# Fifteen expert blocks beside the cross-attention instead of eleven, in groups that sum no batch

## The chip, the cores and the metric

The kernel runs on one core of one Trainium2 chip. The metric is the device time of one execution in microseconds (us); smaller is better. All data is float32. The program is written engine by engine: TensorE (PE) multiplies, ScalarE (ACT) takes exponentials and ReLUs, VectorE (DVE) does the small arithmetic, GpSimd (POOL) issues the DMAs of the expert blocks, and SyncE (SP) the other DMAs. The engines meet through semaphores.

## The reference

One decoder layer over x of 1024 rows by 128, with a context of 6404 rows by 96:

```python
x = x + _L0_attn_ref(_layernorm(x), Wqvk, Wo)                 # 16 heads of 8, causal
x = x + _L0_xattn_ref(_layernorm(x), ctx_768, Wq, bq, ...)    # 16 heads of 8, 6404 keys
x = x + _L0_ffn_ref(_layernorm(x), router_w, router_b, W1, b1, W2, b2)
# the last one: 8 experts, the 2 best of each row, softmax of their two scores as gates
#   h = relu(x @ W1[e] + b1[e])    (128 -> 512);    y = h @ W2[e] + b2[e]    (512 -> 128)
```

## The kernel before

**The cross-attention.** It takes most of the time. Queries are done in two halves of 512. For each half, the 16 heads are taken as 4 quads of 4 heads, and for each quad the keys as 50 tiles of 128. One tile gives 4 PSUM banks of scores (one a head, 128 keys by 512 queries). The banks are exponentiated in *groups*: `GROUPS[1]` has 505 of them, numbered 0 to 504, in the second half of 3 banks each. PE goes through them in `attention`: in turn `group` it waits for the exponential of `group` (`exp_done`), writes the scores of `group + 2` (line 1541), then sums each *batch* (the 4 banks of one tile) that this exponential completed, with the values (line 1577), and then runs what the table `beside` holds for that number. ACT does one exponential a group (line 826) and nothing else there. There are two sets of 3 PSUM banks, so scores are at most two groups ahead of ACT. As a group has 3 banks and a batch 4, in four groups in a row three complete one batch each and the fourth completes none; in the second half the fourth is the one whose number is 2 above a multiple of 4 (with one change of pattern at the end of each quad, groups 304, 371, 437 and 504, which complete two).

**The experts.** The first 512 rows are known after group 237 (`SUMMED_AT`). Their rows are normalised, routed, sorted by expert through DRAM into up to 15 blocks of 128 rows (`BLOCKS`), and each block is multiplied with the weights of its own expert. One block is two steps on PE: *hidden* (`hidden_of_block`, line 1804, 4 products 128x128x128) and *output* (`output_of_block`, line 1811, 4 products). Each is followed by work of another engine: ReLU with bias (`block_relu`, line 1335, on DVE), and a copy (`block_output`, line 1341, DVE). Blocks 0 to 10 (`EARLY` = 11) are done beside the second half of the cross-attention: block j has its hidden step in group `HIDDEN_AT + BLOCK_STEP * j` = 315 + 16 j, its output step 8 groups later. These are all groups that complete a batch. Before them, four steps (`turn_block_rows`) transpose the block rows in groups 297, 301, 305 and 309. Blocks 11 to 14 come after the attention (`late_hidden`, `late_output` on PE; `late_relu`, `late_output` on ACT, lines 878 and 750), in free PSUM banks.

**After the attention.** The second 512 rows have yet to be projected (`project_heads(2, 1, ...)`, line 1679), added to x and normalised on DVE (lines 1030, 916 to 937), transposed (line 1408) and copied (line 1036). PE runs this projection only after the hidden step of block 12. Then come all 8 experts densely on these 512 rows: 32 units of `hidden_units` (line 1868) and `expert_output` (line 1876) in a loop, ReLU on ACT (line 897), scaling by gates and summing on DVE (lines 1393, 1396). `first_half_together` gates and adds the first 512 rows at expert `MEET_AT`.

**Two branches.** Whether the cross-attention may be computed without a running maximum is decided on the chip: `choose` makes a branch of two programs, the one shown by the trace (`attention`) and a general one. In before, both join and the late blocks and dense experts are written once, behind the join.

POOL loads the weights of block j after the output step of block j - 2 (line 722 to 724), alternating between two places in `q_all`; the last two use parts of `k_ring`.

Of the kernel before, what the change touches and what calls it, by code (L numbers as in the profile page):

```python
# [25 lines left out]
P = 128  # L26
# [22 lines left out]
EARLY = 11  # L49
LATE_BANKS = (2, 4, 5, 6)  # L50
# [175 lines left out]
def ctxT_bank(c):  # L226
# [17 lines left out]
B2_AT, COUNT_AT, TURN_AT, HIDDEN_AT = (SUMMED_AT + n for n in (33, 37, 60, 78))  # L244
BLOCK_STEP, OUTPUT_STEP = 16, 8
# [3 lines left out]
MEET_AT = 3  # L249

BLOCK_STEPS = ([("biases", 0), ("counts", 0)] + [("turned", q) for q in range(-(-BLOCKS // 4))] +
               [(what, j) for j in range(EARLY) for what in ("hidden", "output")] + [("hidden", EARLY)] +
               [(what, j + n) for j in range(EARLY, BLOCKS - 1) for n, what in ((1, "hidden"), (0, "output"))] +
               [("output", BLOCKS - 1)])
# [16 lines left out]
def decoder_layer(nc, x, ctx, wqvk, wo_s, wq, bq, wk, bk, wv, bv, wo_x, bo, rw, rb, w1, b1, w2, b2, out):  # L271
    stack = ExitStack()
    with stack:
# [37 lines left out]
        k_space = k_ring[:, 2 * PIECE:2 * PIECE + 4 * HALF].bitcast(F32).rearrange("p (n c) -> p n c", c=HALF)  # L311
# [99 lines left out]
        def bank(b):  # L411
            return psum[:, b, :]
# [13 lines left out]
        for name in (  # L426
# [8 lines left out]
            "block_ps block_done picked experts_made xs_cleared rows_moved weights0 weights1 weights2 weights3 "  # L435
# [32 lines left out]
        OUTPUTS_STORED = ROWS_LOADED + 16 * 3  # L468
        OUTPUTS_BACK = OUTPUTS_STORED + 16 * 2 * 4

        def weights_of(j):

            if j < EARLY + 2:
                return q_space[:, j % 2 * 2], q_space[:, j % 2 * 2 + 1], s[f"weights{j % 2}"], 32 * (j // 2 + 1)
            n = j - EARLY - 2
            return k_space[:, 2 * n], k_space[:, 2 * n + 1], s[f"weights{2 + n}"], 32
# [157 lines left out]
        def _(pool):  # L634
# [63 lines left out]
            def to_experts(fast):  # L698
# [17 lines left out]
                for j in range(BLOCKS):  # L716
                    w1_at, w2_at, loaded, _ = weights_of(j)
                    if 2 <= j < EARLY + 2:
                        pool.wait_ge(s["block_ps"], block_step("output", j - 2))
                    elif j == EARLY + 2 and fast:  # L720
                        pool.wait_ge(L[1]["qk_done"], piece_scored(LOADS - len(PIECES)))
# [8 lines left out]
                pool.wait_ge(s["block_done"], block_step("output", BLOCKS - 1))  # L730
                store(EARLY, BLOCKS - EARLY)
# [5 lines left out]
            def general_cross():  # L737
                load_v_general(1)
                to_experts(False)
# [3 lines left out]
            choose(pool, 1, lambda: to_experts(True), general_cross)  # L743
# [4 lines left out]
        def _(act):  # L748
# [124 lines left out]
            act.wait_ge(s["experts_made"], 2)  # L873

            def late_relu(j):
                act.wait_ge(s["block_ps"], block_step("hidden", j))
                for f in range(NF):
                    ins = act.activation(block_hidden[j % 2][:, f * P:(f + 1) * P], bank(j % 2)[:, f * P:(f + 1) * P],
                                         ACT.Relu, bias=b1_blocks[:, j, f:f + 1])
                ins.then_inc(s["block_done"], 1)  # L880

            def late_output(j):
                act.wait_ge(s["block_ps"], block_step("output", j))
                evac(blocks[:, j, :], bank(LATE_BANKS[j - EARLY])[:, 0:D], s["block_done"])

            late_relu(EARLY)
            for j in range(EARLY + 1, BLOCKS):
                late_relu(j)
                late_output(j - 1)
            late_output(BLOCKS - 1)  # L890

# [512 lines left out]
        def _(pe):  # L1404
# [421 lines left out]
            def late_hidden(j):  # L1826
                if j - 2 >= EARLY:
                    pe.wait_ge(s["block_done"], block_step("hidden", j - 2))
                hidden_of_block(j, bank(j % 2))

            def late_output(j):
                pe.wait_ge(s["block_done"], block_step("hidden", j))
                output_of_block(j, bank(LATE_BANKS[j - EARLY])[:, 0:D])
# [97 lines left out]
```

## Time and profile before

| | |
|---|---|
| time before, median of 3 runs | 978.95 us (977.52 to 982.57) |
| the profiled execution | 975.13 us, span 973.4 us |
| ACT busy | 858.2 us (88%) |
| PE busy | 861.8 us (89%) |
| DVE busy | 183.2 us (19%) |
| POOL busy | 46.7 us (5%) |

The span runs from the first to the last recorded instruction; the execution's own time is 1.7 us longer. "Idle before" is time in which an engine had nothing running before an instruction, and "<-" names what ended it. The granted clock of TensorE is a share of 2.4 GHz: 1.00 is 2.4, and 0.50 is 1.2.

### The profile page before, as it was taken

What the parts mean: (1) busy time and instruction counts of PE and PEld (TensorE: products, weight loads), DVE (VectorE), ACT (ScalarE), POOL (GpSimd) and SP (SyncE); (2) the same over time, 40 slices, a digit from 0 to 9 for tenths busy, and PEclk for the clock granted to TensorE, in tenths of its full rate; (3) what the DMA queues carried; (4) which work ended last, traced back from release to release, by engine and by line L of the source; (5) the groups of instructions that cost most, each with busy time, mean ns of one, the idle gap of its engine ahead of it and who ended that gap; (6) DMA issues with size and microseconds to landing.
All of it is one profiled execution on the core that took longest, in us unless ns stands there. A gap on an engine that the chain in (4) does not pass through costs nothing.

```text
span 973.4 us, 15333 instructions
## 1 busy us (share of the span) xinstructions
PE 861.8 (89%) x6269; PEld 268.6 (28%) x6269; DVE 183.2 (19%) x498; ACT 858.2 (88%) x685; POOL 46.7 (5%) x104
## 2 busy tenths in 40 slices
PE   6977889999888888888889999999999999998997
PEld 3552222222111111111112222222223222222543
DVE  5765643321000000000002220100010001000432
ACT  5667987999999999999999999999999999997432
POOL 4000000000000000000000031000000000010300
PEclk9988999999999999999999999999999999999999
DMA  4252006511112112121111123122322220110120
GB/s 145 109 186 50 2 7 188 156 33 33 36 36 46 38 39 42 40 37 36 33 33 37 36 53 119 36 58 56 63 55 59 61 55 30 44 55 22 34 98 12
DMA packets 24810, 56.13 MB, mean 58 GB/s; under 512 B 6986, under 2 KB 12084, under 8 KB 24476
## 3 DMA queue, kind: packets, MB, share of 16 engines
q1 hardware_dynamic: 21276, 44.18, 17.7%
q0 software_dynamic: 3456, 10.88, 3.8%
q8 instruction: 52, 0.85, 0.4%
q14 instruction: 26, 0.21, 0.1%
HBM read 37.59 MB, written 9.59 MB: 48 GB/s over the span
## 4 chain that ended last, share of the span: by engine, by line
PE 43%; ACT 30%; issue 24%; DVE 2%; DMA 1%; SPq 0%; ACTq 0%; DVEq 0%
ACT probs L826 29%; PE psum L1577 16%; PE psum L1541 10%; PE psum L1868 3%; PE psum L1876 3%; PE psum L1433 1%; PE psum L1811 1%; PE psum L1804 1%; PE psum L1473 1%; PE psum L1477 1%; PE psum L1693 1%; PE psum L1573 1%; PE psum L1460 1%; DVE turned L1064 1%; PE psum L1679 0%
## 5 line engine op out<-in xcount | busy, mean ns | idle before, releaser
L826 ACT ACTIVATE probs<-psum 128x1536 f32<-128x1536 f32 (+1 forms) x553 | 790.9, 1615 | 38.8 <-PE psum L1541 24.2
L1577 PE MATMUL psum<-probs,v_ctx 128*9 128x512 f32 x3200 | 420.4, 597 | 2.7 <-DVE turned L1064 1.9
L1541 PE MATMUL psum<-q_all,k_ring 32*128 32x512 f32 (+1 forms) x1792 | 279.2, 490 | 86.5 <-ACT probs L826 80.3
L1541 PEld LDWEIGHTS psum<-q_all,k_ring 32*128 32x128 f32 x1792 | 107.6, 183 | 466.1 <-ACT probs L826 406.4
L1064 DVE STREAM_TRANSPOSE turned<-psum 128x512 f32<-128x512 f32 x16 | 11.5, 717 | 352.1 <-PE psum L1573 336.9
L1577 PEld LDWEIGHTS psum<-probs,v_ctx 128*9 128x9 f32 x3200 | 47.6, 88 | 103.3 <-issue 97.3
L897 ACT ACTIVATE probs<-psum,b_sb 128x512 f32<-128x512 f32 x32 | 22.0, 687 | 34.6 <-PE psum L1868 34.6
L1577 PE MATMUL psum<-probs,v_self 128*9 128x512 f32 (+3 forms) x384 | 40.4, 520 | 1.8 <-DVE probs L1085 1.2
L703 POOL DMA_INDIRECT block_rows<-xn,slots x8 | 7.9, 983 | 560.8 <-DVE slots L1312 558.6
L1868 PE MATMUL psum<-xnT,w_region 128*128 128x512 f32 x64 | 32.8, 597 | 0.9 <-DVE xnT L1036 0.9
L1876 PE MATMUL psum<-probs,ctx_region 128*128 128x512 f32 x64 | 32.4, 592 | 0.0
L1085 DVE TENSOR_TENSOR probs<-probs,causal 128x384 f32<-128x384 f32 (+2 forms) x53 | 22.8, 476 | 18.0 <-ACT probs L826 17.9
L1341 DVE COPY kparts_bc<-psum 128x128 f32<-128x128 f32 x11 | 3.2, 291 | 102.7 <-PE psum L1811 102.6
L723 POOL DMA_DIRECT2D q_all<-w_region x13 | 7.1, 545 | 269.7 <-issue 269.7
L1335 DVE TENSOR_SCALAR ptail<-psum,b_blocks 128x128 f32<-128x128 f32 x24 | 6.8, 344 | 59.4 <-PE psum L1804 59.4
L1460 PE MATMUL psum<-ident,ctx_region 128*96 128x128 f32 x50 | 8.4, 296 | 9.8 <-DMA ctx_region<-in_ctx 8.2
L1876 PEld LDWEIGHTS psum<-probs,ctx_region 128*128 128x128 f32 x64 | 12.2, 190 | 15.3 <-issue 15.3
L1804 PE MATMUL psum<-kparts_bc,q_all 128*128 128x128 f32 x104 | 14.8, 286 | 1.7 <-issue 1.7
L1335 DVE TENSOR_SCALAR turned<-psum,b_blocks 128x128 f32<-128x128 f32 x20 | 5.6, 344 | 55.5 <-PE psum L1804 55.5
L1868 PEld LDWEIGHTS psum<-xnT,w_region 128*128 128x128 f32 x64 | 11.8, 190 | 15.4 <-issue 14.3
L1804 PEld LDWEIGHTS psum<-kparts_bc,q_all 128*128 128x128 f32 x104 | 12.5, 191 | 12.1 <-issue 12.1
L1477 PEld LDWEIGHTS psum<-wv_sb,w_region 97*128 97x128 f32 x100 | 13.4, 194 | 6.4 <-issue 6.3
(206 smaller groups left out, 395.5 us busy)
## 6 DMA issues: line engine op xcount, KB each, us to landing
k_ring<-kc_parts SPq DMA_DIRECT2D x256, 52.0 KB
k_ring<-kc_parts SPq DMA_DIRECT2D x256, 48.0 KB
kc_parts<-kparts_bc SPq DMA_DIRECT2D x8, 512.0 KB, 2.8
q_all<-w_region POOLq DMA_DIRECT2D x13, 256.0 KB, 2.9
q_all<-ctx_region POOLq DMA_DIRECT2D x13, 256.0 KB, 4.8
kc_parts<-probs SPq DMA_DIRECT2D x4, 512.0 KB, 3.2
w_region<-in_L_ffn_W SPq DMA_DIRECT2D x1, 2048.0 KB, 10.0
probs<-gate_rows SPq DMA_DIRECT2D x2, 1024.0 KB, 5.2
```

The costliest lines, as they stand in the source:

```text
L826: act.activation(probs[:, slot:slot + w, :], psum[:, at:at + w, :], ACT.Exp, scale=SC[ph]).then_inc(L[ph]["exp_done"], 1)
L897: act.activation(hidden[:, n % FFN_RING, :], bank(n % HID_BANKS), ACT.Relu, bias=b1_sb[:, e * NF + f:e * NF + f + 1]).then_inc(s["hid_relu ...
L1064: dve.transpose(turned[:, hf, :], bank(sum_bank(ph, hf, g))).then_inc(L[ph][f"turned{hf}"], 1)
L1085: ins = dve.tensor_tensor(here, here, causal[:, :].unsqueeze(1).to_broadcast([P, n_at, P]), ALU.mult)
L1335: ins = dve.tensor_scalar(block_hidden[j % 2][:, f * P:(f + 1) * P], bank(SIDE_BANK)[:, f * P:(f + 1) * P], b1_blocks[:, j, f:f + 1], 0.0, ...
L1460: mm = pe.transpose(bank(ctxT_bank(c))[0:C, t % CHUNK * P:(t % CHUNK + 1) * P], ctx_sb[:, t, :], ident[:, :])
L1477: mm = pe.matmul(bank(4 + c % 2)[:, t % CHUNK * D:(t % CHUNK + 1) * D], ctxT[:, c % CT_RING, at:at + P], wv_sb[:, :], start=True, stop=True)
L1541: mm = pe.matmul(into[:, col:col + n_q], keys, q_all[rows, g, hf * HALF + q0:hf * HALF + q0 + n_q], start=True, stop=True)
L1577: mm = pe.matmul(into[:, q0:q0 + w], v_all[:, h, t, :], probs[:, place(ph, at)[1], col:col + w], start=first, stop=last)
L1804: mm = pe.matmul(into[:, f * P:(f + 1) * P], w1_at[:, f * P:(f + 1) * P], blocks[:, j, :], start=True, stop=True)
L1868: pe.matmul(bank(n % HID_BANKS), w1_sb[:, e, f * P:(f + 1) * P], xnT[:, HALF:2 * HALF], start=True, stop=True).then_inc(s["hid_ps"], 1)
L1876: pe.matmul(bank(4 + e % 4), w2_sb[:, e, f, :], hidden[:, n % FFN_RING, :], start=(f == 0), stop=(f == NF - 1)).then_inc(s["hid_used"], 1)
```

## The change

`EARLY` becomes `BLOCKS` (15), so the late blocks, their PSUM banks, their weights in `k_ring` and their ACT code go away. The hidden step of block j is in group 314 + 12 j and its output step 4 groups later; the transposing steps are in groups 294, 298, 302 and 306. All of these groups complete no batch. The projection of the second half is the first thing that PE does after the attention. What PE does after the attention is now written twice, once at the end of each branch. `MEET_AT` becomes 0.

```diff
-EARLY = 11
-LATE_BANKS = (2, 4, 5, 6)
+EARLY = BLOCKS
...
-B2_AT, COUNT_AT, TURN_AT, HIDDEN_AT = (SUMMED_AT + n for n in (33, 37, 60, 78))
-BLOCK_STEP, OUTPUT_STEP = 16, 8
+B2_AT, COUNT_AT, TURN_AT, HIDDEN_AT = (SUMMED_AT + n for n in (33, 37, 57, 77))
+BLOCK_STEP, OUTPUT_STEP = 12, 4
...
-MEET_AT = 3
+MEET_AT = 0
...
-            late_relu(EARLY)
-            for j in range(EARLY + 1, BLOCKS):
-                late_relu(j)
-                late_output(j - 1)
-            late_output(BLOCKS - 1)
...
-            choose(pe, 1, lambda: attention(1, first_routed, PART_AT, n_groups(1)), general_cross)
...
-            late_hidden(EARLY)
-            for j in range(EARLY + 1, BLOCKS):
-                late_hidden(j)
-                late_output(j - 1)
-                if j == EARLY + 1:
-                    project_heads(2, 1, wox_sb, CHAIN_BANK)
-            late_output(BLOCKS - 1)
-            transpose_norm(1, 6, CHAIN_BANK)
...
+                project_heads(2, 1, wox_sb, CHAIN_BANK)
+                transpose_norm(1, 6, CHAIN_BANK)
...
+            def fast_cross():
+                attention(1, first_routed, PART_AT, n_groups(1))
+                experts()
...
+            choose(pe, 1, fast_cross, slow_cross)
```

PE's program around block 0, in the second half of the cross-attention (`psum<-q_all,k_ring` are scores, `psum<-probs,v_ctx` the sums of a batch, `psum<-kparts_bc,q_all` a hidden step and `psum<-q_all,ptail` an output step). Before:

```order
L1541 MATMUL psum<-q_all,k_ring 128x512 x6
L1577 MATMUL psum<-probs,v_ctx 9x512 x4
L1804 MATMUL psum<-kparts_bc,q_all 128x128 x4
L1541 MATMUL psum<-q_all,k_ring 128x512 x3
L1577 MATMUL psum<-probs,v_ctx 9x512 x4
L1541 MATMUL psum<-q_all,k_ring 128x512 x3
L1577 MATMUL psum<-probs,v_ctx 9x512 x4
L1541 MATMUL psum<-q_all,k_ring 128x512 x6
```

After:

```order
L1549 MATMUL psum<-probs,v_ctx 9x512 x4
L1513 MATMUL psum<-q_all,k_ring 128x512 x3
L1776 MATMUL psum<-kparts_bc,q_all 128x128 x4
L1513 MATMUL psum<-q_all,k_ring 128x512 x3
L1549 MATMUL psum<-probs,v_ctx 9x512 x4
L1513 MATMUL psum<-q_all,k_ring 128x512 x3
L1549 MATMUL psum<-probs,v_ctx 9x512 x4
L1513 MATMUL psum<-q_all,k_ring 128x512 x3
L1783 MATMUL psum<-q_all,ptail 128x128 x4
L1513 MATMUL psum<-q_all,k_ring 128x512 x3
```

The step stood behind the sums of a batch and now stands between two groups of scores, and the output step follows after two batches more.

PE's program from the last sums of the attention to the first dense expert. Before, from the jump to the joined program on:

```order
L462 UNCONDITIONAL_BRANCH
L1804 MATMUL psum<-kparts_bc,q_all 128x128 x8
L1811 MATMUL psum<-q_all,turned 128x128 x4
L1679 MATMUL psum<-wox_sb,attnT 128x128 x4
L1804 MATMUL psum<-kparts_bc,k_ring 128x128 x4
L1811 MATMUL psum<-q_all,ptail 128x128 x4
L1804 MATMUL psum<-kparts_bc,k_ring 128x128 x4
L1811 MATMUL psum<-k_ring,turned 128x128 x4
L1811 MATMUL psum<-k_ring,ptail 128x128 x4
L1408 MATMUL psum<-ident,xn 128x128 x4
L1868 MATMUL psum<-xnT,w_region 128x512 x2
```

After:

```order
L1549 MATMUL psum<-probs,v_ctx 9x512 x8
L1545 MATMUL psum<-ptail,v_ctx 9x512 x4
L1651 MATMUL psum<-wox_sb,attnT 128x128 x4
L1380 MATMUL psum<-ident,xn 128x128 x4
L1829 MATMUL psum<-xnT,w_region 128x512 x2
```

The four late blocks and the jump are gone from this place; the projection stands right behind the last sums, and only the transposes of the normalised rows stand between it and the dense experts.

## Rows read from the trace of the kernel before

**Rows 1.** The page's busy time by engine, its share of the span, instructions.

```profile
PE 861.8 (89%) x6269; PEld 268.6 (28%) x6269; DVE 183.2 (19%) x498; ACT 858.2 (88%) x685; POOL 46.7 (5%) x104
```

**Rows 2.** Stretches: groups with blocks beside them, and the chain after the attention.

```profile
core 0: us, PE busy (x) PEld busy (x) DVE busy (x) ACT busy (x) POOL busy (x), PEclk, DMA share, GB/s
625.00:894.00 269.00, 247.90 (x1883) 73.71 (x1883) 18.12 (x61) 258.22 (x190) 15.66 (x28) 1.00 0.21 50
894.00:911.00 17.00, 13.07 (x102) 9.63 (x103) 7.70 (x30) 6.22 (x21) 0.79 (x1) 1.00 0.05 19
```

**Rows 3.** ACT's timeline: start, length, instruction, [idle before].

```profile
559.08 52.80 ACT L826 ACTIVATE probs<-psum 128x1536 f32<-128x1536 f32 x39
...
580.60 20.29 ACT L826 ACTIVATE probs<-psum 128x1536 f32<-128x1536 f32 x15
...
614.54 13.54 ACT L826 ACTIVATE probs<-psum 128x1536 f32<-128x1536 f32 x10 [1.02 <-PE psum L1541]
628.49 10.98 ACT L826 ACTIVATE probs<-psum 128x1536 f32<-128x1536 f32 x8 [0.41 <-PE psum L1541]
639.88 10.98 ACT L826 ACTIVATE probs<-psum 128x1536 f32<-128x1536 f32 x8 [0.41 <-PE psum L1541]
651.28 10.99 ACT L826 ACTIVATE probs<-psum 128x1536 f32<-128x1536 f32 x8 [0.42 <-PE psum L1541]
...
709.12 10.99 ACT L826 ACTIVATE probs<-psum 128x1536 f32<-128x1536 f32 x8 [1.27 <-PE psum L1541]
```

**Rows 4.** Timeline of PE and DVE around the hidden step of block 1.

```profile
648.67 1.05 PE L1577 MATMUL psum<-probs,v_ctx 128*9 128x512 f32 x8
649.64 1.16 PE L1804 MATMUL psum<-kparts_bc,q_all 128*128 128x128 f32 x8
650.73 0.50 PE L1541 MATMUL psum<-q_all,k_ring 32*128 32x512 f32 x3
650.84 1.12 DVE L1335 TENSOR_SCALAR turned<-psum,b_blocks 128x128 f32<-128x128 f32 x4 [11.11 <-PE psum L1804]
651.17 1.04 PE L1577 MATMUL psum<-probs,v_ctx 128*9 128x512 f32 x8
...
652.14 0.50 PE L1541 MATMUL psum<-q_all,k_ring 32*128 32x512 f32 x3
```

**Rows 5.** Timeline: a step in a batchless group (PE), block rows and weights (POOL).

```profile
568.85 0.50 PE L1541 MATMUL psum<-q_all,k_ring 32*128 32x512 f32 x3
569.28 0.42 PE L1785 MATMUL psum<-both,causal 128*128 128x40 f32 x2
569.52 1.04 PE L1788 MATMUL psum<-both,ones 128*128 128x32 f32 x8
570.49 0.51 PE L1541 MATMUL psum<-q_all,k_ring 32*128 32x512 f32 x3
...
585.13 1.27 POOL L706 DMA_DIRECT2D kparts_bc<-block_rows  x1 [1.56 <-DMA block_rows<-xn,slots]
595.47 0.62 POOL L723 DMA_DIRECT2D q_all<-w_region  x1 [9.07 <-issue]
```

**Rows 6.** The timeline from the last sums to the first dense unit.

```profile
895.80 1.04 PE L1573 MATMUL psum<-ptail,v_ctx 128*9 128x512 f32 x8
...
898.27 0.71 DVE L1025 STREAM_TRANSPOSE attnT<-heads 128x512 f32<-128x512 f32 x1
898.54 1.86 PEld L1804 LDWEIGHTS psum<-kparts_bc,q_all 128*128 128x128 f32 x16 [2.62 <-issue]
898.57 2.02 PE L1804 MATMUL psum<-kparts_bc,q_all 128*128 128x128 f32 x16 [1.73 <-issue]
...
902.00 1.06 PE L1679 MATMUL psum<-wox_sb,attnT 128*128 128x128 f32 x8
...
903.10 0.69 DVE L1030 TENSOR_TENSOR x_sb<-psum,x_sb 128x512 f32<-128x512 f32 x1 [4.12 <-PE psum L1679]
...
908.70 0.66 PE L1408 MATMUL psum<-ident,xn 128*128 128x128 f32 x4 [0.57 <-DVE xn L937]
...
910.21 1.98 PE L1868 MATMUL psum<-xnT,w_region 128*128 128x512 f32 x4 [0.85 <-DVE xnT L1036]
```

**Rows 7.** DVE's timeline across its own join, after the self-attention.

```profile
149.43 0.29 DVE L1071 TENSOR_TENSOR heads<-turned,rden 128x128 f32<-128x128 f32 x1
150.35 0.71 DVE L1025 STREAM_TRANSPOSE attnT<-heads 128x512 f32<-128x512 f32 x1 [0.63 <-DVE heads L1071]
```

**Rows 8.** Stretches early in the kernel, as in rows 2.

```profile
60.00:70.00 10.00, 5.62 (x55) 4.10 (x52) 7.21 (x17) 5.34 (x12) 0.00 (x0) 0.83 0.55 193
70.00:80.00 10.00, 7.93 (x65) 2.84 (x60) 5.26 (x12) 7.55 (x6) 0.00 (x0) 0.66 0.51 97
```

**Rows 9.** PE's timeline in and after that stretch.

```profile
69.33 0.80 PE L1541 MATMUL psum<-q_all,k_ring 32*128 32x384 f32 x6 [2.97 <-ACT probs L826]
...
72.83 1.90 PE L1577 MATMUL psum<-probs,v_self 128*9 128x512 f32 x8
...
86.77 1.05 PE L1577 MATMUL psum<-probs,v_self 128*9 128x512 f32 x8
```

**Rows 10.** The chain that ended last, in order of time: dense units.

```profile
915.07 0.86 PE psum L1868 x2
915.92 0.86 PE psum L1876 x2
```

More of the change, by code:

```diff
@@ L242 @@
 assert GROUPS[1][SUMMED_AT + 35][1] == 3
-B2_AT, COUNT_AT, TURN_AT, HIDDEN_AT = (SUMMED_AT + n for n in (33, 37, 60, 78))
-BLOCK_STEP, OUTPUT_STEP = 16, 8
+B2_AT, COUNT_AT, TURN_AT, HIDDEN_AT = (SUMMED_AT + n for n in (33, 37, 57, 77))
+BLOCK_STEP, OUTPUT_STEP = 12, 4
+assert all(HIDDEN_AT + n not in {batch_ready(1, m) for m in range(len(PLANS[1][1]))} for m_ in range(EARLY) for n in (m_ * BLOCK_STEP, m_ * BLOCK_STEP + OUTPUT_STEP))
 ROUTER3_AT, LOGITS3_AT, GAP3_AT, GATES3_AT = 1, 3, 4, 7
-MEET_AT = 3
+MEET_AT = 0
 BLOCK_STEPS = ([("biases", 0), ("counts", 0)] + [("turned", q) for q in range(-(-BLOCKS // 4))] +
-               [(what, j) for j in range(EARLY) for what in ("hidden", "output")] + [("hidden", EARLY)] +
-               [(what, j + n) for j in range(EARLY, BLOCKS - 1) for n, what in ((1, "hidden"), (0, "output"))] +
-               [("output", BLOCKS - 1)])
+               [(what, j) for j in range(EARLY) for what in ("hidden", "output")])
 def block_step(what, n=0):
@@ L467, in decoder_layer @@
         ROWS_LOADED = ROWS_PLACED + 16
[L468 removed]
+        OUTPUTS_STORED = ROWS_LOADED + 16 * 2
         OUTPUTS_BACK = OUTPUTS_STORED + 16 * 2 * 4
         def weights_of(j):
[L473 to L476, printed above, removed]
+            return q_space[:, j % 2 * 2], q_space[:, j % 2 * 2 + 1], s[f"weights{j % 2}"], 32 * (j // 2 + 1)
         def raw(c, w=HALF):
@@ L872, in _ @@
             act.wait_ge(s["b_done"], 1)
[L873 to L884, printed above, removed]
-            late_relu(EARLY)
-            for j in range(EARLY + 1, BLOCKS):
-                late_relu(j)
-                late_output(j - 1)
-            late_output(BLOCKS - 1)
             for n in range(E * NF):
@@ L1871, in expert_output @@
-            def expert_output(n):
-                e, f = n // NF, n % NF
-                if f == 0 and e >= 4:
-                    pe.wait_ge(s["y_scaled"], e - 3)
-                pe.wait_ge(s["hid_relu"], n + 1)
-                pe.matmul(bank(4 + e % 4), w2_sb[:, e, f, :], hidden[:, n % FFN_RING, :],
-                          start=(f == 0), stop=(f == NF - 1)).then_inc(s["hid_used"], 1)
-            def output(hf):
-                pe.wait_ge(s["yT_done"], 1)
-                for b in range(4):
-                    mm = pe.transpose(bank(CHAIN_BANK)[:, b * P:(b + 1) * P], yT[:, hf, b * P:(b + 1) * P], ident[:, :])
-                mm.then_inc(s["y_ps"], 1)
@@ L1911, with slow_cross @@
+            def fast_cross():
+                attention(1, first_routed, PART_AT, n_groups(1))
+                experts()
+            def slow_cross():
+                general_cross()
+                experts()
+            choose(pe, 1, fast_cross, slow_cross)
 _NAMES = ["x", "ctx_768", "L0_attn_Wqvk", "L0_attn_Wo", "L0_xattn_Wq", "L0_xattn_bq", "L0_xattn_Wk", "L0_xattn_bk",
```

77 lines of the change are left out of this document (38 added, 39 removed).

## The prediction

> **What bounds the kernel now.** I read the page first: PE and ACT are both busy nearly nine tenths of the span [rows 1], so neither can be called the bound from that alone. The stretches say the same of the 269 us in which the blocks lie: ACT 258, PE 248 [rows 2]. The timeline of ACT decides. Where no step is near, 15 exponentials take 20.29 us with no idle time; less the 1.45 us of one, that is 14 steps of 1.346 us, and I use 1.343. Where block steps lie, ACT runs 8 exponentials, sits idle 0.41 us for the scores of line 1541, and starts again: 639.88, 651.28, so 11.40 us for 8 groups where 8 x 1.343 = 10.74 would do [rows 3]. So ACT is the bound, and each block step (there is one every 8 groups) costs it 0.66 us. After the attention there is a chain that neither engine fills: last sums, block 11, projection, DVE, transposes, first dense unit [rows 6]; after it PE runs dense.
>
> **Why a step costs 0.66.** On PE the scores of a group take 0.43 us to the next instruction (650.73 to 651.17), a batch 0.98 (651.17 to 652.14), a block step 1.09 (649.64 to 650.73) [rows 4]. A group with a batch is 1.41, 0.07 more than ACT's 1.343; a group without is 0.43 and gives back 0.91. PE starts a group about 0.05 behind the end of its exponential; the scores that it then writes are wanted by ACT two groups later, and from the start of scores to the start of their exponential is 0.55 (650.73 to 651.28) [rows 3, 4]. The exponential of group g + 2 then ends at 0.05 + 0.55 + 1.45 = 2.05 behind that of g, plus PE's lateness, and 2 x 1.343 = 2.69 is on time: PE may be 0.64 late. Today a step stands on top of a batch: 0.43 + 0.98 + 1.09 - 1.343 = 1.16 late, then 0.07 and 0.07 more, 1.30, less 0.64 = 0.66. The reckoning gives what the rows show, so I use it for the changed order.
>
> **The steps in the attention.** A step now makes a batchless group of 0.43 + 1.09 = 1.52, so it adds 0.18 instead of 1.16. But one group in twelve alone is left empty. Through twelve groups: three batches 0.20, step 0.38, three batches 0.58, step 0.76, three batches 0.96, and the scores of the empty group start 0.96 late, 0.32 beyond the 0.64. That group then clears all. The sums agree: 12 x 0.43 + 9 x 0.98 + 2 x 1.09 = 16.16 us of PE for 12 x 1.343 = 16.12 of ACT. So PE and ACT are level, and a block costs about 0.3 us instead of 2 x 0.66 = 1.32. Fifteen blocks: 4.5 us; eleven today: 14.5. Gain 10.0. The four transposing steps are short (like the 1.2 us of line 1785 and 1788, which stand in a batchless group at 569.28 and leave ACT's row of 39 exponentials from 559.08 unbroken [rows 3, 5]). Today they stand on batches. From 559.08 (group 268) to 628.49 (group 318) 50 groups take 69.41 us where 67.15 would do [rows 3]: of the 2.3 us, 0.6 belong to block 0, and of the other 1.7 I count 1.1 as won back (bounds 0.3 and 1.7), since the end of a quad, with the idle 1.02 at 614.54, lies in them and stays. Attention: 10.0 + 1.1 = 11.1 us earlier. The bounds are 16 us, if a step cost nothing any more, and -4, if it cost what it costs today; I keep near the reckoning, which meets the one case that the rows can show.
>
> The first transposing step moves from group 297 to 294, whose exponential ends near 595.5. POOL's load of the block rows began at 585.13 and its next instructions, which wait for it, issue at 595.47 after a 9.07 us pause [rows 5]: landed about a microsecond ahead, so no wait. DVE's ReLU of 1.12 us (650.84) has four groups, 5.4 us, to the output step [rows 4]; the weights have 20 groups. Queued behind PE, should either be late, are all the scores, but the cover is large. POOL's stores and gathers now fall into the attention, so `MEET_AT` 0 finds them done: cost nothing, and 2.8 us of DVE work under PE's dense loop.
>
> **The chain behind it.** From the end of the last sums (896.84) to the first dense unit (910.21) are 13.4 us [rows 6]. The attention's transposed output is ready at 898.98. Before, PE projects only at 902.00 and DVE adds at 903.10. Now PE has nothing ahead of the projection: 898.98, 0.05 for the signal, 0.1 for the first weights and 1.06 give 900.2, DVE adds at 900.3, and the rest (903.10 to 910.21) is as long as before: 2.8 us saved. DVE's own jump to its joined program remains; after the self-attention such a one took 0.63 us [rows 7], which fits under the projection. So of the four late blocks, 8 steps of about a microsecond each on PE, only 2.8 us come off: the rest lay beside DVE's chain, 7.1 us, which stays. PE's jump, idle 1.73 us before its first late product [rows 6], is gone too, but behind a wait for DVE that is just as long, so writing the experts twice gives nothing on this path.
>
> **The clock.** The late blocks also kept PE busy while DVE normalised; the clock there is 1.00 [rows 2]. Now PE has nothing from 900.3 to 905.9: 5.6 us of idle time, then transposes of 0.66, and another 0.85. Early in the kernel PE sat idle 2.97 us before 69.33, and the two stretches about it have 0.83 and 0.66 [rows 8, 9]: 10 x (0.17 + 0.34) x 2 = 10.2 us at 1.2 GHz. The same eight passes took 1.90 us there and 1.05 at 2.4 GHz [rows 9]. The gap of 1.73 us at 896.84 did not bring it down [rows 2, 6]. So 5.6 us most likely will. Below, it costs nothing; above, 10.2 us at 1.2 GHz, all in dense work, would cost 5.1. Part lies in the idle time; I take 0.7 for the transposes and some 4.6 us of dense units at 1.2 GHz, 2.3: an estimate of 3.0 in all. The Trainium skill (TensorE: Matmul & The Clock Gate, Part 1) says that an array left idle goes to half rate and that activity releases it; it speaks against taking other work out of such a chain, and the trace agrees with it at 69.33. By that rule the sum is the 968.0 below; by the gap at 896.84 alone it would be 965.
>
> **The sum.** 975.13 - 11.1 - 2.8 + 3.0 = 964.2 for an execution like the profiled one. That one lies 3.8 us under the median of the runs (978.95), and I take the same differences there: 978.95 - 10.9 = 968.0.
>
> **The rivals.**
> - *As forecast*: 968. Chance 0.50; its own range 965 to 971.5.
> - *The clock holds*: 965. For it: the 1.73 us gap was harmless, and transposes and projection break the idleness. Against: rows 8. Chance 0.16.
> - *PE becomes the bound.* 16.16 against 16.12 leaves nothing for a price that I have too low; a step right behind scores may start later than one behind a batch. At 0.15 us more a step the twelve groups lose 0.3 more, 4.5 us in all: 972.5; at 0.25, 975.5. For it: PE has no slack left to recover. Against: line 1785 starts 0.43 behind its scores, as a batch does [rows 5]. Chance 0.21.
> - *Slower: the steps carry over.* If one empty group in twelve does not clear the lateness, all steps cost ACT what today's do: 30 x 0.66 = 19.8 instead of 14.5. Then 978.95 + 5.3 - 1.1 - 2.8 + 3.0 = 983.4. It decides from a loss of 1.03 us in twelve groups (the even point, 10.9 / 15 + 0.3). Nothing in the rows makes it likely, as the reckoning above met today's 0.66. Chance 0.05.
> - *The moves do nothing* (a new wait, as on weights or block rows, eats the gain): 979. Chance 0.08.
>
> **How the numbers follow.** The runs differ by 0.5% among themselves, 977.5 to 982.6, so within 0.5% (974.1 to 983.8) counts as no change. The forecast and the held clock are faster, and two thirds of the PE-bound case: 0.50 + 0.16 + 0.15 = 0.81. Same: the rest of that case, the moves that do nothing and some of the slower case, 0.15. Slower 0.04. The range takes in the held clock with a little beneath it and the PE-bound case: 962.5 to 975.5.
>
> **What would show it.** Right: ACT's idle pieces of 0.41 every 8 groups are gone, and in twelve groups ACT's starts take 16.3 to 16.5 us;  the projection starts within 0.1 us of the transposed output; 10.5 us from the last sums to the first dense unit, and a granted clock below 1.00 in the first microseconds of the dense loop, where a pair of units takes up to 3.4 instead of 1.72 [rows 10]. Wrong: scores that start over 0.64 us late elsewhere than at the twelfth group; a PE wait on weights or on DVE before a block step; a clock of 1.00 throughout.

## The result, and the profile after

| | before | changed |
|---|---|---|
| median of 12 runs each | 980.48 us (977.11 to 986.27) | 976.16 us (972.79 to 980.78) |
| the profiled execution | 975.13 us, span 973.4 | 975.41 us, span 973.7 |
| ratio of the times, 95% | | 0.9957 (0.9938 to 0.9976) |

The change gained 4.3 us where 10.9 were forecast, and 976.16 lies 0.7 us outside the range. The two profiled executions are equally long; but before's is shorter than all twelve of its timed runs (the lowest is 977.11), while the changed kernel's lies among its own. Yet the mechanism in the attention worked as forecast: something else took the time back.

The page's busy times of the changed kernel:

```profile
PE 867.3 (89%) x6269; PEld 270.5 (28%) x6269; DVE 188.6 (19%) x518; ACT 853.0 (88%) x665; POOL 46.0 (5%) x103
```

Against [rows 1], PE does the same 6269 instructions in 5.5 us more, most of it time at the lower clock. ACT has 20 instructions fewer, those of the late blocks, and is 5.2 us less busy.

ACT's timeline of the changed kernel, from the gap's exponential to the end of the attention (start, length, instruction, idle time before it):

```profile
546.95 33.97 ACT L817 ACTIVATE probs<-psum 128x1536 f32<-128x1536 f32 x25
583.77 4.20 ACT L817 ACTIVATE probs<-psum 128x1536 f32<-128x1536 f32 x3 [2.85 <-remote]
588.50 1.45 ACT L817 ACTIVATE probs<-psum 128x1536 f32<-128x1536 f32 x1 [0.53 <-PE psum L1513]
590.14 25.63 ACT L817 ACTIVATE probs<-psum 128x1536 f32<-128x1536 f32 x19 [0.19 <-PE psum L1513]
616.02 1.45 ACT L817 ACTIVATE probs<-psum 128x1536 f32<-128x1536 f32 x1 [0.26 <-PE psum L1513]
617.90 83.11 ACT L817 ACTIVATE probs<-psum 128x1536 f32<-128x1536 f32 x61 [0.43 <-PE psum L1513]
...
880.47 4.14 ACT L817 ACTIVATE probs<-psum 128x1536 f32<-128x1536 f32 x3 [3.56 <-remote]
885.37 1.45 ACT L817 ACTIVATE probs<-psum 128x1536 f32<-128x1536 f32 x1 [0.76 <-PE psum L1513]
887.06 6.40 ACT L817 ACTIVATE probs<-psum 128x1536 f32<-128x1536 f32 x5 [0.24 <-PE psum L1513]
```

Two things stand in it. The pieces of 8 exponentials with 0.41 us of idle time between them [rows 3] are gone: from 617.90 on, 61 exponentials (those that start before 700, where the window ends; the whole piece has 67 in 91.67 us, which gives 1.367) take 83.11 us, so (83.11 - 1.45) / 60 = 1.361 a group or 16.3 us for twelve, as forecast (16.3 to 16.5). But ACT sits idle 2.85 us before 583.77 and 3.56 us before 880.47, each with some smaller pieces behind it, and what ended that time is not an engine that the view can name ("remote"). Before had neither: [rows 3] begin with 39 exponentials in a row from 559.08 on, and its last 19, from 869.55 to 894.88, are unbroken too. I call them the two stalls.

In both it is ACT that stops, and PE then waits for it. The timeline of the changed kernel in the first stall, with PE:

```profile
579.65 0.50 PE L1513 MATMUL psum<-q_all,k_ring 32*128 32x512 f32 x3
...
580.97 0.50 PE L1513 MATMUL psum<-q_all,k_ring 32*128 32x512 f32 x3 [0.82 <-ACT probs L817]
...
583.77 4.20 ACT L817 ACTIVATE probs<-psum 128x1536 f32<-128x1536 f32 x3 [2.85 <-remote]
...
585.27 0.62 PE L1513 MATMUL psum<-q_all,k_ring 32*128 32x512 f32 x3 [2.82 <-ACT probs L817]
```

ACT ended an exponential at 580.92, and the scores for the next were written by 580.15; yet ACT starts it at 583.77. PE needs its end (585.22) and goes on at 585.27. The second stall is alike: scores written by 875.96, ACT free at 876.92 and started at 880.47, PE again at 881.98.

The chain behind the attention, in the timeline of the changed kernel, beside [rows 6]:

```profile
894.37 1.04 PE L1545 MATMUL psum<-ptail,v_ctx 128*9 128x512 f32 x8
...
896.84 0.71 DVE L997 STREAM_TRANSPOSE attnT<-heads 128x512 f32<-128x512 f32 x1
...
897.70 1.13 PE L1651 MATMUL psum<-wox_sb,attnT 128*128 128x128 f32 x8 [2.29 <-DVE attnT L997]
900.40 0.69 DVE L1002 TENSOR_TENSOR x_sb<-psum,x_sb 128x512 f32<-128x512 f32 x1 [2.84 <-issue]
...
906.00 1.11 PE L1380 MATMUL psum<-ident,xn 128*128 128x128 f32 x4 [7.17 <-DVE xn L909]
...
907.97 3.78 PE L1829 MATMUL psum<-xnT,w_region 128*128 128x512 f32 x4 [0.85 <-DVE xnT L1008]
```

The projection starts 0.15 us behind the transposed output (897.55) and ends at 898.83. DVE, however, adds only at 900.40, after 2.84 us of idle time that nothing but its own issuing ended. From the end of the last sums (895.41) to the first dense unit are 12.6 us; it was 13.4, and 10.5 was forecast. The transposes take 1.11 us and the first four passes of dense units 3.78, where they took 0.66 and 1.98 [rows 6]: the clock has come down. The stretches say how far and how long (columns as in [rows 2]; the seventh value is the granted clock):

```profile
core 0: us, PE busy (x) PEld busy (x) DVE busy (x) ACT busy (x) POOL busy (x), PEclk, DMA share, GB/s
...
899.50:913.20 13.70, 6.35 (x10) 1.99 (x10) 5.72 (x26) 1.37 (x2) 0.00 (x0) 0.50 0.01 2
913.20:973.00 59.80, 55.28 (x137) 24.41 (x136) 18.83 (x46) 20.82 (x31) 0.00 (x0) 0.99 0.12 45
```

The granted clock is 0.50, thus 1.2 GHz, for 13.7 us. From the first dense unit to the end of the span are 65.7 us; before, from 910.21 to 973.4, it was 63.2. With the 0.45 of the transposes the clock costs 3.0 us, the size forecast.

### The profile page after: what moved, and what is told of

Its sections match the earlier page's. It is cut to its first block, busy times and chain, and to the rows that moved or that the text cites. A ratio compares the mean times of both kernels' runs of the same rounds, so it can differ in the third digit from the quotient of the medians.

```text
span 973.7 us, 15334 instructions
## 1 busy us (share of the span) xinstructions
PE 867.3 (89%) x6269; PEld 270.5 (28%) x6269; DVE 188.6 (19%) x518; ACT 853.0 (88%) x665; POOL 46.0 (5%) x103
## 4 chain that ended last, share of the span: by engine, by line
PE 54%; ACT 24%; issue 17%; DVE 3%; another core or an unknown queue 1%; DMA 1%; SPq 0%; ACTq 0%; DVEq 0%
ACT probs L817 24%; PE psum L1549 22%; PE psum L1513 13%; PE psum L1829 3%; PE psum L1837 3%; PE psum L1776 2%; PE psum L1783 2%; PE psum L1405 1%; PE psum L1445 1%; PE psum L1449 1%; PE psum L1665 1%; DVE turned L1036 1%; PE psum L1545 1%; PE psum L1432 1%
## 5 line engine op out<-in xcount | busy, mean ns | idle before, releaser
L1307 DVE TENSOR_SCALAR ptail<-psum,b_blocks 128x128 f32<-128x128 f32 x32 | 9.0, 345 | 82.6 <-PE psum L1776 82.6
L1307 DVE TENSOR_SCALAR turned<-psum,b_blocks 128x128 f32<-128x128 f32 x28 | 7.9, 344 | 65.5 <-PE psum L1776 65.5
L1776 PE MATMUL psum<-kparts_bc,q_all 128*128 128x128 f32 x120 | 17.4, 288 | 0.0
L1776 PEld LDWEIGHTS psum<-kparts_bc,q_all 128*128 128x128 f32 x120 | 14.5, 191 | 3.7 <-issue 3.7
```

Source lines behind the costliest of these rows:

```text
L1776: mm = pe.matmul(into[:, f * P:(f + 1) * P], w1_at[:, f * P:(f + 1) * P], blocks[:, j, :], start=True, stop=True)
```

## The experiments

**How the table is read.** Three rows cut each execution up: the first exponential behind ACT's `gap_exp` (for before 546.89), the end of the last exponential of the attention (894.88, the row `869.55 25.33` of ACT's timeline), and the end of the span. The middle piece holds all block steps and is called the attention below; the last is called the tail. These, and the number of stalls, are those of the profiled execution. "Ratio" is that of the run times, with its 95% interval; "beside" is before's median in the same comparison (three comparisons, each on another chip).

| kernel | median us | beside | ratio | attention | tail | stalls |
|---|---|---|---|---|---|---|
| before | 980.48 | | | 348.0 | 78.5 | 0 |
| changed | 976.16 | 980.48 | 0.9957 (0.9938 to 0.9976) | 346.5 | 80.2 | 2 |
| e0_before_again | 974.86 | 975.77 | 0.9995 (0.9979 to 1.0011) | 347.9 | 79.7 | 0 |
| e1_batchless11 | 961.43 | 975.77 | 0.9862 (0.9846 to 0.9879) | 333.3 | 78.5 | 0 |
| e2_gathers_late | 966.53 | 975.77 | 0.9908 (0.9882 to 0.9935) | 337.2 | 80.5 | 0 |
| e3_dve_both | 964.18 | 975.77 | 0.9883 (0.9867 to 0.9899) | 337.3 | 79.0 | 0 |
| f1_after_again | 967.17 | 976.45 | 0.9907 (0.9875 to 0.9939) | 337.2 | 80.6 | 0 |
| f2_filler | 966.66 | 976.45 | 0.9912 (0.9881 to 0.9944) | 337.2 | 81.8 | 0 |
| f3_twelve | 957.02 | 976.45 | 0.9808 (0.9781 to 0.9835) | 333.3 | 75.8 | 0 |
| g1_many_gathers | 966.03 | 975.58 | 0.9898 (0.9871 to 0.9924) | 337.2 | 80.8 | 0 |
| g2_filler5 | 963.87 | 975.58 | 0.9873 (0.9845 to 0.9901) | 337.2 | 75.9 | 0 |
| g3_after_third | 966.43 | 975.58 | 0.9902 (0.9873 to 0.9931) | 337.3 | 80.6 | 0 |
| g4_dve_both_again | 963.85 | 975.58 | 0.9878 (0.9845 to 0.9911) | 337.2 | 79.0 | 0 |

Up to the first of these three rows all kernels do the same work, and yet it lies anywhere from 544.3 to 550.1 us in the thirteen profiled executions. So a difference of a few us is read from the attention and the tail, and not from a span alone.

### First comparison: which part gave what

**e0_before_again** is before, unchanged.

> The kernel before, unchanged, for its trace. In the changed kernel's trace ACT sits idle 2.85 us before group 284, while GpSimd scatters the block rows, a place where both programs are the same; the trace of before has no such idle time. Theory A: that stall comes and goes from execution to execution of either kernel, and the profiled execution of before (975.1 against a median of 980.5) was one without it. Then this trace may show ACT idle 2 to 4 us near 580 us and a span of 977 to 980; without it, 973 to 974. Rival: the stall belongs to the changed program, and this trace has none whatever its span. Ratio to before 1.000 by either.

It came out the same, 0.9995, and its profiled execution has no stall. Its tail, however, is 1.2 us longer than before's. The timeline of e0_before_again behind the last sums:

```profile
898.78 3.08 PE L1804 MATMUL psum<-kparts_bc,q_all 128*128 128x128 f32 x16 [1.95 <-issue]
...
903.17 1.06 PE L1679 MATMUL psum<-wox_sb,attnT 128*128 128x128 f32 x8
```

and a stretch of it (columns as in [rows 2]):

```profile
899.50:903.00 3.50, 3.50 (x19) 3.50 (x18) 0.00 (x0) 2.24 (x8) 0.00 (x0) 0.51 0.02 5
```

The first 16 passes take 3.08 us instead of 2.02 [rows 6], and the projection starts at 903.17 instead of 902.00, because the clock is at 1.2 GHz from 899.5 to 903.0. So it can fall in the unchanged kernel's chain too, behind 1.95 us in which PE is idle.

**e1_batchless11** leaves everything of before in place but moves the steps of the eleven early blocks into groups without a batch, still 16 groups apart.

```diff
-B2_AT, COUNT_AT, TURN_AT, HIDDEN_AT = (SUMMED_AT + n for n in (33, 37, 60, 78))
+B2_AT, COUNT_AT, TURN_AT, HIDDEN_AT = (SUMMED_AT + n for n in (33, 37, 57, 77))
```

> The kernel before with its steps in groups that sum no batch, and nothing else of the change: eleven blocks, hidden steps every 16 groups from 314, output 8 behind, transposing steps from 294. By the reckoning of the prediction a step adds 0.18 us of lateness and three batches 0.20 more, under the 0.64 that PE may be late, so no step costs ACT anything: 22 x 0.66 + about 1 = 15 to 16 us less than before, ratio 0.984 to 0.985. Rival: PE has to pay for its extra work anywhere, as 8 groups hold 9.9 us of PE work in 10.7 us of ACT: then the gain is under 8 us.

The attention is 348.0 - 333.3 = 14.7 us shorter, and the time with it: 14.3 us less, a little under the 15 to 16 expected. Its ACT timeline has unbroken rows as long as the changed kernel's, at a smaller step (the first row is cut where its window ends, at 700):

```profile
612.99 87.42 ACT L826 ACTIVATE probs<-psum 128x1536 f32<-128x1536 f32 x65 [0.43 <-PE psum L1541]
...
792.38 87.00 ACT L826 ACTIVATE probs<-psum 128x1536 f32<-128x1536 f32 x65 [0.69 <-PE psum L1541]
```

(87.42 - 1.45) / 64 = 1.343 is ACT's own pace, so eleven blocks cost nothing. This one line of the change is worth more than the whole change, even where that has no stall (0.9862 against 0.9907 and 0.9902, f1 and g3 below).

**e2_gathers_late** puts POOL's gathers behind the attention again, as a test whether they cause the second stall. Nothing is left out.

```diff
-MEET_AT = 0
+MEET_AT = 3
...
+                if fast:
+                    pool.wait_ge(L[1]["exp_done"], n_groups(1))
                 for n in range(2 * 4):
                     pool.indirect_dma_start(got[n // 4][:, n % 4 * D:(n % 4 + 1) * D], None, ys_dram[:, :],
```

> The changed kernel with GpSimd's eight gathers of the block outputs held back until the last exponential, where before had them, and MEET_AT 3 again. Theory A: the idle 3.6 us of ACT before group 496, and the 1.2 us after it, come from the gathers running beside the attention; they go, and the kernel is 4.5 to 6 us faster than the changed one: 970 to 972, ratio to before about 0.991. Rival (chance or PE's code): the stall stays within a few groups of its place, and the time is that of the changed kernel, ratio 0.996.

No stall, 966.53 us. By itself that looks as if the gathers were the cause of the second; but the stall beside the scatters is gone too, which this edit doesn't touch, and e3 and f1 below keep the gathers where the change puts them and have no stall either. So it doesn't tell.

**e3_dve_both** writes DVE's part behind the attention at the end of both branches, as the change did for PE, so that DVE no longer jumps there.

```diff
-            choose(dve, 1, lambda: normalise(1, first_half_routed), general_cross)
...
+            def fast_cross():
+                normalise(1, first_half_routed)
+                tail()
...
+            choose(dve, 1, fast_cross, slow_cross)
```

(`tail` holds what stood behind `choose` before, word for word.)

> The changed kernel with what DVE does after the attention written at the end of each of its two branches too, so that DVE does not jump before it adds the projection. In the changed kernel's trace DVE's add starts 1.6 us after the projection is done, 2.85 us after DVE's last work. Theory A: that is DVE's jump; the add then starts 0.05 after the projection, and the kernel gains 1.4 to 1.8 us on the changed one, ratio to before 0.994. Rival: DVE waits for something else (the clock of PE, a late signal), and nothing changes: 0.996.

The timeline of e3_dve_both at the place where the changed kernel has 2.84 us of idle time:

```profile
887.61 1.28 PE L1660 MATMUL psum<-wox_sb,attnT 128*128 128x128 f32 x8 [2.29 <-DVE attnT L997]
889.00 0.69 DVE L1002 TENSOR_TENSOR x_sb<-psum,x_sb 128x512 f32<-128x512 f32 x1 [1.54 <-PE psum L1660]
```

DVE now waits for PE alone, and the add comes 1.4 us behind the projection's start instead of 2.7. From the transposed output to the add are 1.5 us (887.46 to 889.00) where it was 2.85, so the jump costs 1.3 there; the tail is 79.0 here and in g4, and 80.2 to 80.8 in the five profiled executions with the jump, thus 1.2 to 1.8 longer.

### Second comparison: the change once more, a filler, and a better version

**f1_after_again** is the changed kernel, unchanged.

> The changed kernel unchanged, on another chip than its first twelve runs. In the last runs a kernel with the same ScalarE, TensorE and GpSimd programs up to the last exponential had neither of the two stalls of the changed kernel's trace (ACT idle 2.9 us before group 284, 3.6 us before group 496), though its gathers ran beside the attention too. Theory B: the stalls belong to that chip or those executions, not to the program; here they are absent, the span is 973.7 - 4.2 - 5.0 = 964 to 966 and the ratio 0.989 to 0.991. Rival (theory A, gathers beside the attention): the stalls are there again, near 580 and 878 us, and the ratio is 0.995 to 0.997.

It gained 9.3 us (0.9907), not 4.3. Its ACT timeline at the two places of the stalls (two windows of one timeline; a row is cut where its window ends):

```profile
568.89 32.48 ACT L817 ACTIVATE probs<-psum 128x1536 f32<-128x1536 f32 x24
...
853.77 30.82 ACT L817 ACTIVATE probs<-psum 128x1536 f32<-128x1536 f32 x23
```

ACT is unbroken in both, and the attention takes 337.2 us. The same program has 346.5 in the execution profiled with the result: the stalls and what follows from them cost 9.3 us there. The medians differ by as much: 976.16 less the mean of f1 and g3 (966.8) is 9.4.

**f2_filler** is e3 with 12 useless products on PE between the projection and the transposes. They write a PSUM bank that nobody reads, and are meant to keep the clock up.

```diff
                 project_heads(2, 1, wox_sb, CHAIN_BANK)
+                for n in range(12):
+                    pe.matmul(bank(0), wox_sb[:, :], xnT[:, 0:HALF], start=True, stop=True)
                 transpose_norm(1, 6, CHAIN_BANK)
```

> The changed kernel with DVE's last part in both branches (as the run with the ratio 0.9883), and 12 products of 128x128x512 written by PE between the projection and the transposes, into a PSUM bank that nothing reads: work without use, 12 x 0.43 = 5.2 us, to fill the time in which DVE normalises. Theory: the clock of 0.5 from 888 to 902 in that run is what PE's idleness of some 6 us costs, 3.0 us; with the filler the clock stays at 1.00 and the kernel is 2.5 to 3.3 us faster, ratio 0.985 to 0.986. Rival: the clock falls anyway, or what it costs is hidden, and the ratio stays 0.988; if the filler delays the transposes, it is slower.

The timeline of f2_filler between projection and dense units:

```profile
886.71 12.16 PE L1857 MATMUL psum<-xnT,wox_sb 128*128 128x512 f32 x24
...
898.71 0.60 PE L1389 MATMUL psum<-ident,xn 128*128 128x128 f32 x4
...
900.16 1.98 PE L1838 MATMUL psum<-xnT,w_region 128*128 128x512 f32 x4 [0.85 <-DVE xnT L1008]
```

Here a product counts as two passes (x24 for 12 instructions), so the filler ran 12.16 us, more than twice the 5.2 that I had reckoned, and DVE's rows were ready 6 us before the transposes (898.71). Transposes and dense units ran at full clock (1.98 for the four passes). But the filler did not keep the clock from falling, as a stretch at its beginning shows (columns as in [rows 2]):

```profile
886.90:890.40 3.50, 3.50 (x5) 1.35 (x5) 3.11 (x16) 0.00 (x0) 0.00 (x0) 0.51 0.02 5
```

PE is busy all through it at half clock. The fall comes 0.2 us into the filler, behind the 2.29 us of idle time in front of the projection. The filler made the low stretch shorter, 3.4 us where the changed kernel has 13.7, but the tail is 81.8: too much filler gives nothing back.

**f3_twelve** joins what had paid: before with e1's table, one more block beside the attention (`EARLY` 12, so three late blocks), the projection right behind the first late hidden step, and PE's and DVE's last parts in both branches.

```diff
-EARLY = 11
-LATE_BANKS = (2, 4, 5, 6)
+EARLY = 12
+LATE_BANKS = (2, 4, 5)
...
+                late_hidden(EARLY)
+                project_heads(2, 1, wox_sb, CHAIN_BANK)
```

> Meant to beat both: the steps 16 groups apart in groups without a batch (which cost ACT nothing), so 12 blocks beside the attention and three after it; after the attention the hidden step of the first of the three, then the projection, then the rest of the three while DVE normalises; PE's and DVE's last parts in both branches. Against the kernel with 11 such blocks (ratio 0.9862, span 957.9): the chain from the last sums to the first dense unit shortens from 13.4 to 10.5 to 11 us and the clock stays at 1.00: 955 to 955.5, ratio 0.983 to 0.984. Rival: the three blocks behind the projection delay the transposes, or the twelfth block costs ACT its 1.3 us: ratio 0.986 or more.

It is the fastest of all, 957.02 us, 0.9808, and beats both kernels. Its timeline behind the attention:

```profile
881.14 1.16 PE L1813 MATMUL psum<-kparts_bc,q_all 128*128 128x128 f32 x8
...
883.41 1.16 PE L1688 MATMUL psum<-wox_sb,attnT 128*128 128x128 f32 x8 [1.11 <-DVE attnT L1025]
...
884.67 0.69 DVE L1030 TENSOR_TENSOR x_sb<-psum,x_sb 128x512 f32<-128x512 f32 x1 [1.32 <-PE psum L1688]
...
888.48 1.16 PE L1820 MATMUL psum<-k_ring,ptail 128*128 128x128 f32 x8 [0.34 <-ACT ptail L878]
...
890.28 0.66 PE L1417 MATMUL psum<-ident,xn 128*128 128x128 f32 x4 [0.64 <-DVE xn L937]
...
891.78 1.98 PE L1877 MATMUL psum<-xnT,w_region 128*128 128x512 f32 x4 [0.85 <-DVE xnT L1036]
```

The last sums end at 881.21 and the first dense unit starts 10.6 us later, as I had forecast for the change (10.5). Three late blocks fill PE while DVE normalises, they delay nothing, and in this execution the clock stays at full rate (1.98). The means of the granted clock in its six runs, 0.985 to 0.988, fit the same in the others (e3's five have 0.979 to 0.985). The twelfth block cost nothing: the attention takes 333.3 us, as in e1. The tail is 75.8, 2.7 under before's: the chain's gain without the clock's cost.

### Third comparison: the stalls, and a filler of the right size

**g1_many_gathers** is the changed kernel with 104 more indirect loads of block rows, eight after each of the first 13 output steps. They read rows that nobody uses. If indirect transfers beside the exponentials cause stalls, this has many.

```diff
                     if j >= 2:
                         pool.wait_ge(s["block_ps"], block_step("output", j - 2))
+                        for n in range(8):
+                            at = n % 4 * D
...
+                            pool.indirect_dma_start(got[0][:, at:at + D], None, xs_dram[:, :],
+                                                    bass.IndirectOffsetOnAxis(slots[:, n:n + 1], 0)).then_inc(s["extra_rows"], 16)
```

> The changed kernel with eight extra gathers by GpSimd after the output step of each of the first 13 blocks: they read rows of the block input from DRAM into a place that the last eight overwrite, so they are work without use, some 130 us of indirect DMAs beside the attention. Theory C: the stalls of ACT and PE come from indirect DMAs that run beside the attention, at a low rate on some chips; with 14 times as many, one or more show in the trace, as ACT idle for 2 to 4 us and PE waiting for ACT, and the median rises by 4 us or more over the changed kernel's. Rival: the indirect DMAs have no part in it, no such idle time, and the median is within 1.5 us of the changed kernel's.

Its timeline of POOL (the first row here is one of the 104):

```profile
639.90 0.94 POOL L719 DMA_INDIRECT heads<-block_rows,slots  x1 [4.62 <-DMA heads<-block_rows,slots]
```

Its timeline of ACT:

```profile
613.10 91.67 ACT L824 ACTIVATE probs<-psum 128x1536 f32<-128x1536 f32 x67 [0.45 <-PE psum L1520]
705.20 89.25 ACT L824 ACTIVATE probs<-psum 128x1536 f32<-128x1536 f32 x65 [0.43 <-PE psum L1520]
```

No stall; 966.03 us, the same as the changed kernel beside it (g3, 966.43). Indirect transfers alone are not the cause.

**g2_filler5** is e3 with 5 products of filler instead of 12 (the same edit with `range(5)`), again useless work in an unused bank.

> As the filler before but with 5 products of 128x128x512 in place of 12. One takes 0.86 us, twice what I had put down, so that 12 of them ran 10.3 us and held the transposes back by some 6 us, while the time did not grow. 5 take 4.3 us in the 5.6 us that DVE needs. Theory: the clock stays at 1.00 behind them, and the kernel is 2.5 to 3.3 us faster than the same without filler (ratio 0.988): 0.985 to 0.986. Rival: the fall of the clock costs nothing that a filler could give back, ratio 0.988.

Its timeline at the same place:

```profile
892.51 4.46 PE L1857 MATMUL psum<-xnT,wox_sb 128*128 128x512 f32 x10
...
898.38 0.66 PE L1389 MATMUL psum<-ident,xn 128*128 128x128 f32 x4 [1.41 <-DVE xn L909]
...
899.89 1.98 PE L1838 MATMUL psum<-xnT,w_region 128*128 128x512 f32 x4 [0.85 <-DVE xnT L1008]
```

Here the timeline shows what was wanted: transposes and dense units at full clock, nothing delayed, a tail of 75.9 against 79.0 in g4_dve_both_again, so the low clock costs 3.1 us. That the filler held it up is not shown: f2 runs the same program as far as the fifth product, and there the clock fell before the first was done. The times don't show a gain either: 963.87 against 963.85. In the profiled execution the head (up to the exponential behind `gap_exp`) is 550.10 - 546.96 = 3.1 us longer than g4's: 2.5 of it is there by 167 us, the rest lies about a stretch from 385 to 395, with a granted clock of 0.66 where g4 has 0.87. Whether its other runs have this too, and why, I can't say; that the low clock costs 3 us is shown in the traces, that this filler saves them in the time is not.

**g3_after_third** and **g4_dve_both_again** are the changed kernel and e3_dve_both once more.

> The changed kernel unchanged, for a third look, on the chip on which the next three run. Its first twelve executions had a mean granted clock near 0.974 and the ratio 0.9957, the next six 0.979 and 0.9907, one of them 971.6 us at 0.974. Theory B: without stalls 0.990 to 0.992; the stalls are events of single executions and chips, and an execution that has them is 4 to 9 us longer at a clock lower by 0.003 to 0.005, of before too. Rival A: 0.995 to 0.997 again.

> The changed kernel with DVE's last part in both branches, again, beside the changed kernel on one chip. Theory: DVE's add starts 1.4 to 1.6 us sooner behind the projection (1.38 us of idle time in front of it instead of 2.8), so 1.5 us less than the changed kernel. Rival: the 3 us between their medians of 967.2 and 964.2 on two chips were more than that, and 2.5 to 3.5 us are seen here too.

g3 gained 9.2 us (0.9902) without a stall. g4 is 2.6 us faster than g3; the tails account for 1.6 of it (80.6 to 79.0), the heads for 0.5, and the rest is within what runs differ by.

## Why the prediction was wrong

**ACT is the bound and a step on a batch costs 0.66: right.** e1 takes eleven blocks and the transposing steps off the batches and gets 14.7 us. The reckoning had 14.5 for the blocks alone today, and 1.1 for the transposing steps, 0.9 too much in all.

**Block steps in batchless groups, every 12: right.** Forecast -11.1 us; the attention is 348.0 - 337.2 = 10.8 us shorter in f1 (10.7 and 10.8 in the others). A block costs (337.2 - 333.3) / 15 = 0.26 us if e1 counts as free; I had 0.3. PE did not become the bound, and the steps did not carry over: those two rivals fall. ACT's 0.43 and 0.63 of idle time at the quads' ends stayed, as they did in e1.

**The chain: wrong in one term.** The step that failed is "DVE's own jump to its joined program remains; after the self-attention such a one took 0.63 us [rows 7], which fits under the projection." It left DVE idle for 2.84 us, and the projection covers only the first 1.3. Without the low clock's 0.45 the chain became 13.37 - (12.56 - 0.45) = 1.3 us shorter instead of 2.8. Of the 1.5 that are missing, e3, which takes only the jump away, gets 1.3 back at the add; the rest is that the add comes 1.5 us behind the transposed output even without the jump, and not 1.3. One row of a short branch early in the program was no bound for this jump: PE's jump at the same join left 1.73 us idle [rows 6], and that row was mine to set beside it, though even it is 1.1 short of what DVE lost. The Trainium skill (Runtime: NRT & Kernel Launch, Instruction fetch mechanics) says that a taken branch to a place outside the pages already fetched waits for the fetch; it gives no price. Removing the jump removed the wait here, in agreement with it, while the length is this trace's.

**The clock: right in what it cost, too simple in what brings it down.** Forecast 3.0, measured 3.0 (0.45 in the transposes, 2.5 behind the first dense unit), and 3.1 from the other side (g2 against g4). All seven profiled executions of kernels with neither late blocks nor filler have 13.7 us at 1.2 GHz there, so the rival that the clock holds falls. But the forecast put the fall down to the 5.6 us behind the projection and took the gap before PE's late work for harmless. In e3 the clock falls at 888.4, before the projection ends (888.89), in f2 with no gap behind it at all, and in e0, the kernel before, behind 1.95 us. Idle time of that size in front is thus enough in some executions (not in before, e1 and g2), and by these executions what PE does next decides how long it lasts: 3.4 us with work (e0, f2), 13.7 without.

**Work at no cost: right.** Stores and gathers in the attention and `MEET_AT` 0 cost nothing in f1 and g3; PE shows no wait on weights or block rows. The microsecond of margin that the forecast gave the block rows is not in its rows, though, which have 595.47 against "near 595.5".

**The sum, with these sizes.** 975.13 - 10.8 - 1.3 + 3.0 = 966.0; f1's profiled execution has a span of 965.2 and thus takes about 966.9 us. The program's own gain over before is 9.2 to 9.3 us, in two comparisons, not 10.9: the 1.5 missing in the chain are nearly all of the difference.

**From the sum to the median: wrong, and this took the forecast out of its range.** "That one lies 3.8 us under the median of the runs (978.95), and I take the same differences there" assumes that what lies between a good execution and the median is alike for both kernels. With the result, before's median was 980.48 and not the 975.6 to 976.5 of the other comparisons, 4.5 us more; the changed kernel's was 9.4 us above its own 966.8. So 4.9 of the 6.6 us by which the gain fell short lie here, and the other 1.7 in the program's own gain. The changed kernel's profiled execution shows where its 9.4 are: two stalls, 346.5 - 337.2 = 9.3 us. The other runs have no trace, but eleven of the twelve have a mean granted clock of 0.968 to 0.975, as that one (0.974), and the twelfth, the fastest (972.79), 0.980; f1's and g3's ten have 0.977 to 0.984, but for one of 971.58 us with 0.974. So the stalls, or something as long, most likely stood in nearly all runs of the first comparison, and perhaps now and then in a later one. That before had about one of the same kind in a typical run there is an inference from its 4.5 us; its profiled execution had none.

**What the stalls are stays open.** The first is at a place where both programs are the same, beside POOL's scatters. The second lies beside the gathers, which the change brought into the attention. That each has eight indirect transfers beside it speaks for them, but e3, f1, g3 (gathers in place, no stall) and g1 (104 more, no stall) show that they don't suffice. In the first, the DMA engines were hardly busier. The stretch of three microseconds in the first stall of the changed kernel (columns as in [rows 2]):

```profile
core 0: us, PE busy (x) PEld busy (x) DVE busy (x) ACT busy (x) POOL busy (x), PEclk, DMA share, GB/s
580.50:583.50 3.00, 1.48 (x11) 0.31 (x11) 0.00 (x0) 0.42 (x1) 2.39 (x3) 1.00 0.18 57
```

The same stretch of before:

```profile
core 0: us, PE busy (x) PEld busy (x) DVE busy (x) ACT busy (x) POOL busy (x), PEclk, DMA share, GB/s
580.50:583.50 3.00, 2.70 (x22) 0.61 (x22) 0.00 (x0) 3.00 (x4) 2.39 (x3) 1.00 0.16 51
```

ACT, and PE behind it, stand still for much of it (0.42 and 1.48 us busy against 3.00 and 2.70) while POOL issues the same three transfers and the DMA share is 0.18 against 0.16. Whether another place of the gathers would remove the second stall on an occasion that has stalls could not be tried: none of the three later comparisons had one in its profiled executions.

## What to carry to other kernels

Put side work into the turns in which the feeding engine has slack, and no more often than its lateness can clear in between: steps every 16 groups were free, every 12 they cost 0.26 us a block. Don't empty the engine that a serial chain elsewhere leaves idle: three late blocks in that gap cost nothing, and the tail was 3 us shorter, at full clock (f3, 75.8, against e3, 79.0). Where code behind a branch is written twice, do it for every engine on the chain: here the one that still jumped set the time. And profile a kernel more than once: a stall or a fall of the clock that one execution has, the next of the same program may not have.

## What the runs showed of the hardware

- A jump to code behind a join left DVE idle for 2.84 us in the changed kernel (900.40) and in f1, and for 2.98, 3.09 and 3.32 in g1, g3 and e2, while the same kind of jump after the self-attention took 0.63 [rows 7]. PE's left it idle for 1.73 [rows 6], and for 1.95 in e0. Its length has to be measured at its place.
- ACT can leave an exponential standing for about three microseconds although its scores are written (583.77), with PE waiting behind it, in one execution of a program that shows none of it in two others (f1, g3); two of these cost 9.3 us, the clock's fall behind them included (0.82 in the stretch of the changed kernel behind the first, columns as in [rows 2]):

```profile
583.70:593.00 9.30, 7.57 (x47) 1.53 (x47) 0.00 (x0) 8.51 (x7) 1.57 (x2) 0.82 0.45 139
```

- A float32 product of 128x128 by 512 columns stands in the timeline as two passes and takes 0.89 us at full clock (4.46 for five, g2); I had reckoned half of it for the filler.
- The granted clock fell to 0.50 behind idle gaps of PE of about 2 us: 1.95 in e0, 2.29 in f2 and in all seven kernels without late blocks or filler. It did not after 1.73 (before), nor after 2.29 in g2. With PE busy behind the gap it was low for 3.4 us (e0, f2); with a second gap of 5.7 to 7.7 us behind the projection, for 13.7 us in all seven.
